# Head pairs in reciprocals and 32x32 transpositions, W1 products evicted with their bias and one gelu, and a group's softmax beside the feed-forward part of the group ahead

## What is computed

```
# layer 0: queries from x (64 rows), keys and values from [ctx; x] (128 rows), 16 heads of 16
q = latents @ q_w + q_b;  kv = concat([ctx, latents]) @ kv_w + kv_b
attn = softmax(where(mask, q k^T / 16, -inf))
y = rmsnorm(attn v @ out_w + out_b + latents) * postnorm_w
x = gelu(y @ mlp_w1 + mlp_b1) @ mlp_w2 + mlp_b2 + latents
# layer 1: over channels (64), 8 heads, 256 positions against 256 positions of ctx
xn = (x - mean) * rsqrt(var + 1e-5) * gamma + beta
q = Wq xn + bq;  k, v = Wkv ctx + bkv
out = x + Wo (softmax(q k^T / 8) v) + bo
```

## Time and profile before

| | |
|---|---|
| median of 3 runs | 671.29 us (670.06 to 671.63) |
| the profiled execution | 670.9 us, span 669.1 us |
| mean granted TensorE clock | 0.962 of full speed |
| busy: PE, PEld, DVE, ACT, POOL | 590.7, 471.7, 575.9, 491.9, 402.8 us |
| first layer-1 scores on TensorE | 97.0 us from the start |
| from 196.67 to 500.28 us | four equal stretches of 75.9 us, one for each group of four batches |

### The profile page before, as it was taken

How to read it: one execution, slowest core, us unless ns; L and a number is a source line. 1 busy time by engine, 2 the same in 40 slices (tenths; PEclk the granted TensorE clock), 3 DMA queues, 4 the chain that set the end, 5 groups by cost and what they waited for, 6 DMA issues and landing times.

```text
span 669.1 us, 21092 instructions
## 1 busy us (share of the span) xinstructions
PE 590.7 (88%) x8436; PEld 471.7 (70%) x8436; DVE 575.9 (86%) x1358; ACT 491.9 (74%) x1875; POOL 402.8 (60%) x392
## 2 busy tenths in 40 slices
PE   3597798799899989999899989999899989898985
PEld 3487776687688767776678667877678767676763
DVE  4685689699978999699987999799987999689993
ACT  1655777868787876878777876879778777867781
POOL 0520438477648857577548857578547857467672
PEclk9777997899999999999999999999999999898987
DMA  9700000011111111111111021111101121010110
GB/s 270 149 33 2 32 18 2 17 30 50 29 41 35 28 45 47 27 42 38 29 42 33 25 49 26 50 41 34 26 16 34 26 50 26 17 26 18 31 37 9
DMA packets 49826, 26.46 MB, mean 40 GB/s; under 512 B 37792, under 2 KB 48064, under 8 KB 49728
## 3 DMA queue, kind: packets, MB, share of 16 engines
q1 hardware_dynamic: 49728, 25.11, 14.6%
HBM read 22.99 MB, written 2.10 MB: 38 GB/s over the span
## 4 chain that ended last, share of the span: by engine, by line
PE 44%; DVE 40%; ACT 8%; DMA 3%; issue 2%; POOL 2%; SPq 1%
PE bank L561 42%; DVE nm L998 10%; DVE E1b L1007 8%; DVE nm L862 4%; DVE hm L882 4%; ACT E1b L1135 3%; DVE QS L991 2%; DMA E1b<-in_w 2%; ACT E L1065 2%; PE bank L681 2%; DVE ZS L1013 1%; ACT hm L1104 1%; DVE rs L1003 1%; DVE aos L808 1%; DVE xnb L983 1%
## 5 line engine op out<-in xcount | busy, mean ns | idle before, releaser
L1192 POOL TENSOR_TENSOR E1b<-E1b,rs 128x512 f32<-128x512 f32 x256 | 267.1, 1066 | 104.4 <-DVE rs L1003 100.4
L1135 ACT ACTIVATE E1b<-bank,nm 128x256 f32<-128x256 f32 x512 | 237.6, 499 | 72.9 <-DVE nm L998 72.6
L1007 DVE STREAM_TRANSPOSE E1b<-E1b 128x512 f32<-128x512 f32 x256 | 170.3, 688 | 2.7 <-POOL E1b L1192 1.9
L998 DVE TENSOR_REDUCE nm<-bank 128x2 f32<-128x512 f32 x256 | 165.4, 672 | 5.3 <-PE bank L561 4.7
L561 PE MATMUL bank<-E1b,CT 32*64 32x256 f32 x4096 | 124.2, 390 | 21.7 <-ACT E1b L1135 10.2
L561 PE MATMUL bank<-ctx,QS 64*128 64x256 f32 x1024 | 139.0, 400 | 3.2 <-ACT QS L1125 1.6
L561 PEld LDWEIGHTS bank<-E1b,CT 32*64 32x64 f32 x4096 | 98.3, 136 | 42.6 <-ACT E1b L1135 12.2
L1135 ACT ACTIVATION_READ_ACCUMULATOR E1b<-bank,nm 128x1 f32 x512 | 118.1, 231 | 0.0
L561 PEld LDWEIGHTS bank<-ctx,QS 64*128 64x128 f32 x1024 | 93.6, 190 | 28.6 <-issue 6.9
L1065 ACT ACTIVATE E<-bank,nm 128x128 f32<-128x128 f32 x256 | 90.4, 405 | 19.6 <-DVE nm L862 19.6
L1162 POOL TENSOR_TENSOR E<-E,rs 128x512 f32<-128x512 f32 x56 | 58.9, 1055 | 39.0 <-DVE rs L868 38.8
(11 more groups left out here) (103 smaller groups left out, 785.1 us busy)
## 6 DMA issues: line engine op xcount, KB each, us to landing
CT<-in_hT SPq DMA_DIRECT2D x256, 32.0 KB, 1.8
hraw<-in_hT SPq DMA_DIRECT2D x8, 512.0 KB, 3.2
ctx<-in_ctx SPq DMA_DIRECT2D x16, 256.0 KB, 3.9
xnat<-in_xn SPq DMA_DIRECT2D x8, 256.0 KB, 2.7
E1b<-in_w SPq DMA_DIRECT2D x2, 1024.0 KB, 11.7
out<-y SPq DMA_DIRECT2D x16, 128.0 KB, 1.8
E1b<-in_kvw SPq DMA_DIRECT2D x2, 256.0 KB, 4.4
mski<-in_msk SPq DMA_DIRECT2D x32, 1.0 KB
```

Of the source, the lines that this page charges most:

```text
L998: e.tensor_reduce(nm1[:, u % 16, :], bank[place["S", u]][:, :].rearrange("p (i t) -> p i t", i=2), AX.X, ALU.max, negate=True).then_inc(dv ...
L1007: e.transpose(E1b[:, u % 16, :, :], E1b[:, u % 16, :, :]).then_inc(dve_steps, 1)
L1135: t = e.activation(E1b[:, r, i, :], bank[bk][:, i * 256:(i + 1) * 256], ACT.Exp, bias=nm1[:, r, i:i + 1], scale=1.0, accum_out=sum1[:, r, ...
L1192: e.tensor_tensor(E1b[:, u % 16, :, :], E1b[:, u % 16, :, :], rs1[:, u % 16, :].unsqueeze(2).to_broadcast([128, 2, 256]), ALU.mult).then_i ...
```

## The change

The reciprocal `N` and the block transposition `U` take two heads at once (128x4 and 128x1024 in place of twice 128x2 and 128x512); `Np` stays one unit an instruction. The W1 products are added to their bias when they leave PSUM (step `W1e`, ScalarE or VectorE, one bank each as soon as it is done), and one `gelu` of 128x2048 in SBUF follows. `PT0` gets memory of its own, so the softmax of a group no longer waits for `gsp` of the group ahead; `yy` shares the memory of `xo`, and `ctx` is loaded for two batches at a time into three buffers. `hlo` may run on GpSimd, the mask row becomes a step `mk` of its own, `xo` is cut into the rounding (`xo`, ScalarE or VectorE) and the subtraction (`xol`, GpSimd or VectorE). The first loads of `CT` wait for `yy` of the first group. The planner gets slower matmuls at the start, a cost for an activation table load, other quotas, wider windows, and shifts for every head, part and first group.

```diff
-NP = ('POOL',)
-WIN = (-22.6, 12.0)
-PREP = 9
-LATE = (-4, -3, 2, 0, 0.5, 4, 3, 3)
-STAY = 1.5
-PREFER = (0, 0)
-QUOTA = dict(S=6, Z=4, other=6)
-HEADAT = -40
-MARGIN = 1
+COLD = (60000, 1.6)
+TABLE, LOAD = dict(gelu="gelu", E="exp", sexp="exp"), 1290
+WIN = (-47.4, 23.4)
+PREP = 15
+LATE = (-4, -3, 3, -4, 0, 4, 4, 4)
+STAY = 0.6
+PREFER = (0, 1)
+QUOTA = dict(S=8, Z=4, other=6)
+HEADAT = -80
+KEEP = 2
+SPARE = 0
+MARGIN = 2
...
-        add("hlo", g, on=A, at=at(), after=[("hhi", g), None if g else ("m0",)] + (
+        add("hlo", g, on=G + A, at=at(), after=[("hhi", g)])
+        add("mk", g, on=A, at=at(), after=[("lh", g) if g else ("m0",)] + (
             [("s", g - 2, c) for c in range(2)] if g >= 2 else []))
...
-                add("t", g, c, r, on=V, at=at(0.4), after=[("snp", g, c, r), prev("o", p1)] + (
-                    [("gsp", g - 1, k) for k in range(4)] if g else []), banks=[("t", g, c, r)], kind="other")
+                add("t", g, c, r, on=V, at=at(0.4), after=[("snp", g, c, r), prev("o", p1)], banks=[("t", g, c, r)], kind="other")
...
-        add("xo", g, on=A, at=at(), after=[("o1", g, c) for c in range(2)] + ([("O", g - 1)] if g else []))
+        add("xo", g, on=P + A, at=at(), after=[("o1", g, c) for c in range(2)] + ([("O", g - 1)] if g else []))
+        add("xol", g, on=G + A, at=at(), after=[("xo", g)])
...
-            add("W1", g, c, on=V, at=at(1.4), after=[("yed", g), ("W1", g, c - 1) if c else None] + [("w1", k) for k in range(4)],
-                banks=[("W1", g, k) for k in range(4)] if c == 0 else [], kind="other")
+            add("W1", g, c, on=V, at=at(1.4), after=[("yed", g), ("w1", c)],
+                banks=[("W1", g, c)], kind="other")
+            add("W1e", g, c, on=P + A, at=at(), after=[("W1", g, c), ("gsp", g - 1, c) if g else None],
+                empties=(("W1", g, c), "other"))
+        add("gelu", g, on=P, at=at(), after=[("W1e", g, c) for c in range(4)])
...
-            add("N", u, on=A, at=u + LATE[3], after=[("E", u)])
-            add("Np", u, on=NP, at=u + LATE[4], after=[("N", u)])
-            add("U", u, on=A, at=u + LATE[5], after=[("Np", u)])
+            if h % 2:
+                add("N", u - 1, on=A, at=u + LATE[3], after=[("E", u - 1), ("E", u)])
+                for i in (u - 1, u):
+                    add("Np", i, on=G, at=i + LATE[4], after=[("N", u - 1)])
+                add("U", u - 1, on=A, at=u + LATE[5], after=[("Np", u - 1), ("Np", u)])
...
-        yy = sb("yy", [128, 2, 256])
+        yy = xo
...
-        PT0 = hm[:, :, :].rearrange("p (r k) n -> p r (k n)", r=4).rearrange("p r (j t) -> p r j t", j=4)
...
-                    if n >= 2:
-                        w.wait_ge(*done("Z", n - 2))
+                    w.wait_ge(*(done("Z", n - 2) if n >= 2 else done("yy", 0)))
...
-                    w.wait_ge(*done("E", u))
-                    e.reciprocal(rs1[:, u % 16, :], sum1[:, u % 16, :]).then_inc(dve_steps, 1)
+                    k = u % 16
+                    w.wait_ge(*last([("E", u), ("E", u + 1)]))
+                    e.reciprocal(rs1[:, k:k + 2, :], sum1[:, k:k + 2, :]).then_inc(dve_steps, 1)
...
-                    w.wait_ge(*done("Np", u))
-                    e.transpose(E1b[:, u % 16, :, :], E1b[:, u % 16, :, :]).then_inc(dve_steps, 1)
+                    k = u % 16
+                    w.wait_ge(*last([("Np", u), ("Np", u + 1)]))
+                    e.transpose(E1b[:, k:k + 2, :, :], E1b[:, k:k + 2, :, :]).then_inc(dve_steps, 1)
```

More of the change, by code:

```diff
@@ L85, in order @@
         free = {e: 0 for e in engines}
-        mode = "full"
+        mode, table = "full", "exp"
         idle = [(0, b, None) for b in range(8)]
@@ L408, in build @@
         X1 = [sb(f"X1{i}", [128, 256]) for i in range(4)]
-        ctx = [sb(f"ctx{i}", [128, GB, 256]) for i in range(2)]
+        ctx = [sb(f"ctx{i}", [128, 2, 256]) for i in range(3)]
         st6 = sb("st6", [128, 6])
@@ L676, in _ @@
                     w.wait_ge(*done("snp", g, c, r))
-                    if g:
-                        w.wait_ge(*last([("gsp", g - 1, k) for k in range(4)]))
                     pb = take("t", g, c, r)
```

162 lines of the change are left out of this document (106 added, 56 removed), and 42 rows, old and new, of tables (COST, SHIFT).

## The result

The changed kernel takes 641.75 us (median of 4 runs, 637.85 to 646.41), the kernel before, run on the same chip, 671.44. The ratio is 0.9565, with a 95% interval of 0.950 to 0.963: 29.7 us less. The forecast was 29.5 less, 641 us. The profiled execution took 637.85 us with a span of 636.1, 33.0 less than the span before.

The account below looks back on a forecast made before the run. TensorE and VectorE, both nearly full, each set part of a group. Terms of -16.2 (196.67 to 580 us), -8.0 (99 to 196.67), -4 (start) and -1.3 (end) give -29.5 from 670.9: 641 us, 8-in-10 range 620 to 666.

Parts of the forecast that it names:

- Groups: Four-batch groups in the middle: 75.9 to 72.7 us each, by switches -0.6 and idle -2.6; -16.2 us over 5.05 groups.
- The four that I named: TensorE's waits in a group: bank freed by ScalarE 0.59, scaling for t 0.60, O 1.00, Z 0.93; 3.1 us.
- the three switches fewer: TensorE's middle groups: 38 switches between kinds of array use become 35, about 0.2 us each, -0.6 us a group.
- VectorE's work: VectorE's busy time in a group: savings less added evictions and scaling give -3.7 us, 69.9 to 66.2.
- rival C: VectorE stays the bound, GpSimd blocking takes back two thirds of its 3.7 us; 653 to 654 us; chance 0.22.
- The gelu at nothing: Between W1 and W2: long gelu and table loads cost nothing, covered by 8 us of TensorE's work.
- The start: 0 to 99 us: hlo on GpSimd brings the first matmul 2.5 us earlier; -4 in all.
- Second stage and end: 99 to 196.67 us: switches -0.8, idle -3.5, moved matmuls -3.7, together -8.0; 580 to 669 us: -1.3.
- A: Rival: the longer pair chain is exposed, each Z up to 1.6 us later; 692 us, half exposed 667; chance 0.10.
- D: Rival: nothing to see, 7.5 us from switches and moved matmuls lost to half-exposed chains; 669 to 673 us; chance 0.04.
- B: Rival: TensorE's idle time goes almost wholly, since matmul busy time holds slack and VectorE bounds; 623 us; chance 0.16.
- My theory that the order brings it: Set for the experiments: the gain comes from TensorE's waits going through the step order, not from VectorE's lighter work.

Follow-up runs that it names:

- experiment 2: Changed kernel with two half-width instructions for each wide reciprocal and transposition, same order and waits: 647.34 us, ratio 0.964.
- experiment 8: Kernel of experiment 1 with the subtraction hlo of group 0 back on VectorE right behind hhi in place of GpSimd: 636.49 us, ratio 0.9464.
- experiment 4: Changed kernel with a second ScalarE pass, an in-place copy of hm, behind each group's gelu, values unchanged: 657.08 us, ratio 0.9792.
- experiment 1: Changed kernel with the mask row of group 1 moved behind the first four softmax maxima on VectorE: 633.83 us, ratio 0.9442.
- 6: Changed kernel, order kept, with 19 of ScalarE's 28 evictions of t in groups 1 to 7 put on VectorE: 647.11 us, ratio 0.962.
- 7: Changed kernel, order kept, with all evictions of t and W1 of groups 1 to 7 on ScalarE: 651.58 us, ratio 0.9673.
- 12: Changed kernel's operations, planner numbers tuned further, first mask row priced at 12 us, xop of group 0 behind the fourth scaling: 627.19 us, ratio 0.9351.
- experiment 5: Changed kernel's new operations with the planner's old numbers, except the new window for layer 0: 679.07 us, ratio 1.0095.

## Why the prediction was right, point by point

- **The number.** That 641 was met to 0.8 us is in part luck. Between the profiled executions the terms came to -33.0 in place of -29.5, and they miss in both directions: 3.8 us too much hoped for up to the first layer-1 scores and 1.6 in the second stage, 3.7 too little in the four equal groups and 5.3 behind them. The profiled execution is also 3.9 us under the median.
- **Groups.** Predicted 72.7 us with 2.0 idle; measured 71.85 with 1.98. The size of the idle time is as forecast, the waits only in part. The four that I named went from 3.12 to 1.33: `O` without a wait, one `Z` at 0.34, the 0.59 for ScalarE gone, but the waits for GpSimd's scaling up from 0.60 to 0.99, where I had half of them go. Some 1.4 us of TensorE's idle time before had no releaser in the profile and no place in my list, and they went too, while 0.75 came in at W2 and behind the eviction of `Z`. The other 0.85 us lie in TensorE's busy time: 71.28 to 69.87, -1.4 where the three switches fewer were put at -0.6. That term was mis-sized. No run parts the switches from the rest of it.
- **VectorE's work.** Predicted 66.2 us, measured 68.40: this step failed. By experiment 2 the wide forms, reciprocals included, are worth 1.2 us where I had 2.6, which is 1.4 of the 2.2 missing. From start to start a wide transposition does hold VectorE for the 1.14 that I took (284.33 to 285.47; the 1225 ns run on into the next instruction), but a narrow pair in experiment 2 holds it for 1.20 and not 1.22, and the joined reciprocals bring less than 1.3. The rest is blocking, some 3 us of it, against shorter steps such as the mask row (633 ns for 1125) and two maxima fewer inside the cut: a `gs` rounding 1006 ns (419 before), `hhi` 1466 (685), `hlo` 1792 (1193), the scaling on VectorE 1344 (0.94 on average). That is rival C's mechanism; C had 2.5 us come back in a group, and 2.2 did, from both causes. But C drew from it that the group would fall by 1.8 us only and the time be 653, and that didn't follow: the group fell by 4.1. VectorE itself stands idle for 3.45 us in a group where it stood for 6.03. The Trainium skill, "SBUF — State Buffer", Who interferes with whom, names conversions as well among the instructions that can be shut out by GpSimd for its whole length; experiment 8 agrees (2.60 us against 0.42).
- **The gelu at nothing.** The sum came out, with less room than I gave it. I had 8 us of TensorE's work against 4.4 of chain. Measured, it is 8.75 against 7.7 (261.1 to 268.8): ScalarE's earlier work ahead of the eviction (0.6), the table load ahead of the gelu (1.28), two softmax exponentials (0.9 together), an eviction of `Z` (0.35) and the evictions of W1 as two instructions on ScalarE were missing. So of experiment 4's next 1.9 us the larger part was exposed at once. The table loads took 1283 ns each. The Trainium skill, "ScalarE: Activation LUTs", What ACT_TABLE_LOAD costs, puts a switch at 2.66 us with a drain; the row of the timeline has the gelu right behind the load, and no drain of that size shows ahead of it.
- **The start.** Predicted -4 up to the first layer-1 scores, measured -0.2. Two steps failed. The subtraction on GpSimd held VectorE's rounding, so the first matmul came at 8.48, not 7.5. And the mask row's place on VectorE, which the lists showed and my working passed over, cost 5.7 us in the trace (experiment 1). Without it the term would have been -5.9.
- **Second stage and end.** Predicted -8.0 and -1.3; measured -6.4, and from 500.28 us on -9.9 where the sum had some -4.6 with the last group's share. In the second stage idle time fell by 4.5 (-3.5 forecast), but the 3.7 us of matmuls that were to leave it did not: it has 1185 matmuls where it had 1128, and TensorE's busy time fell by 1.9 only, with a higher clock. Layer 0 runs further ahead than I counted: the group behind the four equal ones has 9.2 us less of TensorE's work. The end itself gave nothing (96.42 to 96.66): TensorE has 2.1 us less to do there and is idle for 2.4 more.
- **The clock.** My sum has no term for it, and part of the gain outside the equal groups goes with it: 0.95 to 1.00 in the second stage and 0.91 to 0.95 at the end. Between 99 and 140 us a W1 matmul took 322 ns on average before and 285 after. In the four equal groups the clock is 1.00 in both, so their 16.5 us are free of it. Whether the smaller idle time raised the clock is not shown. The slowest run of the changed kernel, at a mean clock of 0.960 (before: 0.962), is still 25 us under the kernel before.
- **Rivals.** A (`Z` exposed) did not come: in the four equal groups one `Z` of four waits, for 0.34 us. C's blocking came, but not its price; D fell with the result. B's argument from weight loads isn't borne out: they are busy for 55.5 of 71.85 us, but TensorE's matmul time in a group stays between 69.4 and 70.2 us in the changed kernel and in experiments 2, 6, 7 and 12, whatever VectorE has to do, and the shortest group is 70.84.
- **Where the gain comes from.** The operations in an order from the old numbers: +9.5 us. One order tuned for the old operations: +0.9, within the measurement. Both: -30. In these lists the gain is in neither part by itself. My theory that the order brings it was half right. My reading is that with the new operations VectorE has room (67 us busy in 78, experiment 5) and that the order then keeps ScalarE from setting the pace in its place; that is argued from these two windows, not tested. Nor is it shown which of the new operations the order needs. The wide forms are worth 0.75 us a group. The looser ties (`PT0` in memory of its own, one bank of W1 at a time, three `ctx` buffers) and the work that changed engines were never taken out one at a time.

## What to carry over

When two engines are both nearly full, lighter instructions on one of them pay only with an order that uses the room; time the new operations in the old order too before a gain is put down to them. Look through the first dozen instructions of each engine's list for a wait on a late DMA: one step in the wrong place cost about 1% here, and it stood in the list. When a forecast is a sum, check it term by term: this one met the total while its parts missed by up to 5 us. Before a long instruction is costed at nothing, write out all that stands on its engine between its input and its consumer, table loads and other steps too.
